# Moving the FFN's scaled float16 copy from ScalarE to GpSimd in a fused attention + FFN kernel

## The reference

```
xn = (x - mean) / sqrt(var + 1e-5)
attention: z = layernorm(xn)*g + b;  q = z Wq + bq, k = q, v = z Wv + bv
           16 heads of 16 channels; softmax(q k^T / 4) v;  times Wo, + bo
ffn:       h = gelu(xn ternary(W1) + b1)        256 -> 1024
           h ternary(W2) + b2                   1024 -> 256
```

## Time and profile before

| | us |
|---|---|
| median of 3 runs | 1436.96 (1436.22 to 1437.12) |
| profiled execution, device time | 1435.52 |
| its span, first to last instruction | 1433.7 |
| TensorE busy | 1384.6 (97%) |
| VectorE busy | 1339.1 (93%) |
| ScalarE busy | 1247.3 (87%) |
| GpSimd busy | 113.7 (8%) |

### The profile page before, as it was taken

The page is one execution under the profiler, slowest core; times in us unless marked ns, Lnnn a source line. Parts: engine busy times, 40 slices in busy tenths (PEclk is TensorE's granted clock), DMA queues, the critical chain, the costliest instruction groups (busy, mean ns, idle before and its releaser), DMA issues.

```text
span 1433.7 us, 32248 instructions
## 1 busy us (share of the span) xinstructions
PE 1384.6 (97%) x13414; PEld 447.5 (31%) x13414; DVE 1339.1 (93%) x1430; ACT 1247.3 (87%) x2284; POOL 113.7 (8%) x246
## 2 busy tenths in 40 slices
PE   7899987999999999999999999999999999999999
PEld 5666542222222222222222222222222222222244
DVE  7868779999999999999999999999999999999934
ACT  5554643999999999999999999899999999999975
POOL 2000005000000000000000000000222200002200
PEclk8999999999999999999999999999999999999999
DMA  6012000010000000100000001001212101001122
GB/s 232 16 36 76 30 16 1 28 31 30 31 31 31 30 31 30 31 30 26 29 30 29 32 29 33 28 32 35 60 61 61 61 31 33 32 33 60 39 100 81
DMA packets 28531, 60.69 MB, mean 42 GB/s; under 512 B 6200, under 2 KB 11736, under 8 KB 28130
## 3 DMA queue, kind: packets, MB, share of 16 engines
q1 hardware_dynamic: 27810, 56.99, 11.8%
q10 hardware_dynamic: 576, 1.65, 0.3%
HBM read 41.29 MB, written 16.77 MB: 40 GB/s over the span
## 4 chain that ended last, share of the span: by engine, by line
DVE 71%; PE 23%; ACT 2%; DMA 2%; issue 1%; POOL 0%; SPq 0%; ACTq 0%; DVEq 0%
DVE part_max L839 68%; PE ps L367 6%; PE ps L384 3%; PE ps L1070 3%; PE ps L1139 3%; PE ps L330 2%; PE ps L1085 2%; PE ps L458 1%; DVE w L831 1%; ACT w L1020 1%; DMA rows<-in_rows 1%; PE ps L439 1%; ACT hidden L1015 1%; PE ps L1111 1%; ACT w L1049 1%
## 5 line engine op out<-in xcount | busy, mean ns | idle before, releaser
L1049 ACT ACTIVATE w<-ps 128x512 f32<-128x512 f32 x2048 | 1111.4, 596 | 63.8 <-PE ps L384 21.6
L839 DVE TENSOR_REDUCE part_max<-ps 128x1 f32<-128x1024 f32 x1024 | 1164.8, 1211 | 1.9 <-PE ps L330 1.7
L367 PE MATMUL ps<-w,v_ones 128*32 128x256 f32 (+1 forms) x7688 | 628.6, 399 | 0.4
L384 PE MATMUL ps<-qry,key 50*128 50x512 f16 x1984 | 411.4, 388 | 7.2 <-ACT w L1049 7.0
L330 PE MATMUL ps<-qry,key 48*128 48x512 f16 x2048 | 404.2, 380 | 11.4 <-DVE part_max L839 11.3
L367 PEld LDWEIGHTS ps<-w,v_ones 128*32 128x32 f32 x7688 | 152.2, 108 | 384.7 <-issue 211.5
L384 PEld LDWEIGHTS ps<-qry,key 50*128 50x128 f16 x1984 | 101.1, 93 | 440.7 <-ACT w L1049 412.5
L330 PEld LDWEIGHTS ps<-qry,key 48*128 48x128 f16 x2048 | 101.5, 95 | 36.8 <-DVE part_max L839 26.4
L638 POOL COPY v_ones<-v_all 128x128 f32<-128x128 f32 x64 | 18.6, 291 | 743.9 <-PE ps L367 743.9
L1011 ACT ACTIVATE q_split<-ps,sigma_bq 128x512 f16<-128x512 f32 x16 | 11.0, 687 | 65.2 <-PE ps L1085 65.2
L1070 PE MATMUL ps<-w_ternary,w 128*128 128x256 f16 x512 | 61.7, 277 | 6.2 <-DVE w L831 6.2
(11 more groups left out here) (144 smaller groups left out, 466.2 us busy)
## 6 DMA issues: line engine op xcount, KB each, us to landing
key<-q_parts SPq DMA_DIRECT2D x64, 128.0 KB
qry<-q_parts SPq DMA_DIRECT2D x64, 128.0 KB
o_heads<-o_evacuated SPq DMA_DIRECT2D x31, 256.0 KB, 10.2
resid<-in_x SPq DMA_DIRECT2D x8, 512.0 KB, 13.8
q_parts<-q_split SPq DMA_DIRECT2D x16, 256.0 KB, 2.5
key<-q_parts SPq DMA_DIRECT2D x64, 64.0 KB
qry<-q_parts SPq DMA_DIRECT2D x64, 64.0 KB
out<-resid SPq DMA_DIRECT2D x7, 512.0 KB, 3.1
```

The costliest lines, as they stand in the source:

```text
L367: mm = eng.matmul(pv[32 * c:32 * c + 2 * D, c0:c1], vst[:, kb, :], prob[kb % 2][:, c * BANK + c0:c * BANK + c1], start=(kb == 0), stop=(kb ...
L384: eng.matmul(ring_bank(v, i, False), key[v][r:r + KROWS, kb * P:(kb + 1) * P], qry[v][r:r + KROWS, c * BANK:(c + 1) * BANK], start=True, s ...
L839: dve.tensor_reduce(part_max[h % 2][:, a // 2, a % 2:a % 2 + 1], pa[a % 2], AX.X, ALU.max).then_inc(s_r, 1)
L1049: act.activation(prob[kb % 2][:, c * BANK:(c + 1) * BANK], ring_bank(k, i, last), ACT.Exp, scale=exp_scale).then_inc(s_e, 1)
```

## The change

ScalarE's 32 copies at L1020, with their waits, are taken out. GpSimd writes the same float16 copy with a `tensor_scalar` multiplication by the column `hs`, one for each pair of blocks, and signals the same semaphore `s_h1`. Its stream is put in a new order: in the loop over the groups, `rsqrt(g + 1)` comes first, then the four copies of group g; the two `stage` copies of head 0 follow those of group 4. VectorE's, TensorE's and SyncE's streams stay as they are.

```
+            def hidden_part1(g):
+                for i in range(KF // 2):
+                    pool.wait_ge(s_g, KF * g + 2 * i + 2)
+                    if g == 0 and i == 0:
+                        pool.wait_ge(s_wd, 4)
+                    pool.tensor_scalar(hp[0][:, 2 * i:2 * i + 2, :], hid[:, 2 * i:2 * i + 2, :], hs[:, 0:1], None,
+                                       ALU.mult).then_inc(s_h1, 1)
...
-            for g in range(1, NG):
-                rsqrt(g)
...
-            pool.wait_ge(s_vd, 2 * NG // NB)
-            stage(0, 0)
-            stage(0, 1)
+            for g in range(NG):
+                if g + 1 < NG:
+                    rsqrt(g + 1)
+                hidden_part1(g)
+                if g == NG // NB:
+                    pool.wait_ge(s_vd, 2 * NG // NB)
+                    stage(0, 0)
+                    stage(0, 1)
             split_max(0)
...
                     act.activation(hid[:, f, :], pf[f % 2], ACT.Gelu, scale=1.0 / XS, bias=b1_col[:, f:f + 1]).then_inc(s_g, 1)
-                    if f % 2:
-                        if first and f == 1:
-                            act.wait_ge(s_wd, 4)
-                        act.wait_ge(s_g, KF * g + f + 1)
-                        act.activation(hp[0][:, f - 1:f + 1, :], hid[:, f - 1:f + 1, :], ACT.Identity,
-                                       scale=hs[:, 0:1]).then_inc(s_h1, 1)
```

## The result

The changed kernel takes **1464.35 us** (median of four runs, 1463.86 to 1466.55) against 1436.59 on the same chip: +27.8 us, a ratio of 1.0196 with a 95% interval from 1.0178 to 1.0214. The forecast was 1440.3, the range 1435 to 1462. The profiled execution of after took 1466.55 us; its span is 1464.6 against 1433.7.

The account below looks back on a forecast made before the run. The prediction took group 0 as bound by VectorE, groups 1 to 3 by the Gelu-and-copy chain, groups 4 to 6 by a chain leaving at Gelu 5. Terms 2.5 + 0.3 + 0.3 + 0.2 = +3.3 us gave 1440.3, range 1435 to 1462.

Parts of the forecast that it names:

- What bounds the kernel: First 240 us: TensorE sees 0.7 us of the copy tail in groups 1 to 3; VectorE is group 0's chain.
- The price of the added instruction: GpSimd's float32-to-float16 tensor_scalar of 128x1024: taken as 1.1 us, between bounds of 1.04 and 2.13 us.
- Who meets whom: GpSimd copies and VectorE's second parts, both using SBUF, would run in turn; each group 0 meeting costs VectorE up to 0.85 us.
- Groups 1 to 3: FFN down +0.1 us later each, +0.3 in all: 0.5 us won on ScalarE is lost in taking turns.
- Order and queues: GpSimd's new order costs nothing: 17.9 us idle before each pow on the mean, 9 left even at 2.13 a copy.
- Groups 4 to 7: Second part 2 +0.1 us later in each of groups 4 to 6, +0.3; two such links in group 7, +0.2.
- Group 0: Copies beside VectorE's norm, ternary weights and second parts: three meetings counted, +2.5 us; 0 at the lower end.
- the first: Rival for all eight groups: arithmetic rate, 2.13 us a copy in turn with second parts, +27 us, 1464; chance 0.13.
- a rival: Faster: second part reaches TensorE's limit, group 0's FFN down loses its 1.3 us low-clock stretch; -3.5 us, 1433.5; chance 0.05.

Follow-up runs that it names:

- e11: Kernel before, idle matmuls ahead of group 0's FFN down and transposes behind groups 4 to 6, third-pair copy of groups 1 to 3 as GpSimd tensor_copy, scale 1: 1429.75 us.
- e1: Kernel before, with one extra GpSimd instruction in each of seven heads where GpSimd is idle, results unread, to price each alone: 1433.35 us, run once.
- e2: Changed kernel with hidden scale set to 1 and a plain tensor_copy on GpSimd instead of the tensor_scalar: 1437.62 us against 1436.22 for the kernel before.
- e8: Changed kernel with scale 1 and tensor_copy on GpSimd, each pair copied twice, first to a scratch: 1465.69 us, ratio 1.0219.
- e12: Changed kernel with scale 1 and tensor_copy on GpSimd, two scratch fills that read nothing ahead of each copy: 1476.09 us, ratio 1.0285.
- e9: Changed kernel with 28 idle matmuls on TensorE ahead of FFN down of groups 1 to 3 only: 1461.01 us.
- e4: Kernel before, with only group 0's four float16 copies moved to GpSimd: 1438.58 us against 1436.22, ratio 1.0016.
- e3: Changed kernel, with group 0's four float16 copies back on ScalarE: 1460.39 us.
- e10: Kernel before, with 24 idle matmuls ahead of FFN down of group 0 and 12 ahead of the transposes behind groups 4 to 6: 1431.78 us against 1436.09.
- e5: Changed kernel with 28 idle matmuls on TensorE ahead of FFN down of groups 0 to 5: 1466.89 us.

## Why the prediction was wrong

- *What bounds the kernel*: right. The tail of 0.7 us in groups 1 to 3 was what could be had (e11 has 0.46 of it a group), and VectorE was the chain of group 0.
- *The price of the added instruction*: **the step that failed.** "I take 1.1, near the cast, because the new instruction too reads one tensor with those types" is wrong, and so is the upper bound of 2.13: I had taken two inputs as the costliest case. By itself the instruction takes 2852 ns (e1). With the price that I had assumed e2 is at +1.4 us (interval -0.9 to +3.2) where the sum said +3.3: within the forecast's own range, though not term by term, as group 0 lost 2.0 in place of 2.5 and got 1.3 back from the clock.
- *Who meets whom*: right in kind. In e8 second part and copy each wait for the other by 0.75 to 0.87 us, near the 0.85 of streaming time that I had priced. It was the wrong place to look: in groups 1 to 3 GpSimd's time for a pair and the slow start behind it give the whole loss (e12).
- *Groups 1 to 3*: said +0.1 each. With the cheap copy -0.2 (e2), with the real one +4.6 in groups 2 and 3: 3.0 of waiting for GpSimd, shown by e9 with the clock kept, and 1.6 for the clock. In group 1 it is +1.7, because FFN down of group 0 had been slow before and is not now.
- *Order and queues*: right that the new order costs nothing (e2). But the 9 us that even 2.13 us a copy would leave were counted over a whole group, and the copies only fit between Gelu 1 and FFN down.
- *Groups 4 to 7*: said +0.5, measured 16.5 in the profile, of which 5.1 are the clock (2.6, 1.4 and 1.2 above). That copies of 2.83 us put the chain on the first copy instead of Gelu 5 follows from the price. How much VectorE's stretched second parts (2.13 and 1.68 us in the chain of group 4) add was not tried apart. e12 without them, at 3.0 us a pair, took 11.7 us from Gelu 1 to the transposes, the changed kernel 11.5; an estimate from these two is 11.7 - 3 x 0.17 = 11.2 without the stretch, so 0.3 of the 2.1 us of a group.
- *Group 0*: said +2.5; FFN down came 3.4 late, and e4 gives +2.4 for it alone in the time of the kernel. Here the meetings are the cause: the four instructions for `xn`, 1.39 us in the earlier trace rows, took 2.88, and the four for `zn`, 1.29 before, took 2.85, together 3.0 of the 3.4.
- *Rivals*: the first gave 1464 and the time is 1464.35, by sums that agree partly by chance: it had a pair at 2.13 + 1.43 = 3.56 us in turns; measured were 2.83 without turns, group 0 at 3.4 in place of 6.5, the lower clock on top, and groups 4 to 7 dearer than it said. The estimate from the GPSIMD Engine Reference of the Trainium skill (Performance versus the Vector engine), 1.54 us by 1.8 cycles an element, was nearer than mine, but still about half of what e1 shows; its advice to keep elementwise arithmetic off this engine is borne out here (2852 ns against the 1148 of ScalarE).
- *TensorE's clock* stood only in a rival, as a gain that needed a shorter pause ahead of FFN down of group 0. That gain of 1.3 us came: the pause was 0.75 us, because VectorE's delay now fell ahead of the transposes, and these began slowly (8 of them in 1.94 us, 1.04 in the earlier trace rows):

```profile
40.94 1.94 PE L1116 MATMUL ps<-ident_f,xn 128*128 128x128 f32 x8 [5.30 <-DVE out_bound L821]
...
47.12 7.16 PE L1075 MATMUL ps<-w_ternary,w 128*128 128x256 f16 x64 [0.75 <-DVE w L842]
```

As a loss, some 8.5 us in groups 2 to 6 of the profiled execution, the clock had no term in the sum.

## What to carry to other kernels

Before work is moved to an idle engine, that engine's price for the very operation has to be known: a row of another operation with the same shapes and types can be off by 2.7 times, and one run with the instruction placed where the engine idles gives it. What counts then is the instruction's time against the time between two of them: with a copy of 1.04 us, less than the 2.4 us between pairs of Gelus, all the waiting on each other cost nothing that the time of the kernel shows (e2), while at 2.83 and 3.0 us each tenth counted four times a group. That the engine idles for half of the group does not help, when its work has to fit into one part of it. A pause ahead of a stage of matmuls can have a second price, a slow start behind it; it did not come each time (in e3 FFN down of group 3 took 7.16 us behind a pause of 3.7 us, those of groups 1 and 2 took 8.83 behind the same). Filling pauses with idle matmuls won 4 us in e10, and put 3 us into the chain where there was no pause (e5).

## What the runs showed of the hardware

The `tensor_scalar` on GpSimd takes 2852 - 1565 = 1287 ns for 512 more elements, 2.5 ns an element, three times the 0.83 of the copy. Why the multiplication is so slow no run shows. The timeline of group 0 in after shows when it keeps VectorE's norm waiting:

```profile
30.12 2.85 POOL L632 TENSOR_SCALAR w<-hidden,hidden_scale 128x1024 f16<-128x1024 f32 x1
...
30.24 1.14 DVE L734 TENSOR_SCALAR xn<-resid,mean_var,rstd 128x256 f32<-128x256 f32 x1 [0.30 <-POOL rstd L621]
31.30 0.72 DVE L734 TENSOR_SCALAR xn<-resid,mean_var,rstd 128x256 f32<-128x256 f32 x2
...
31.95 1.17 DVE L734 TENSOR_SCALAR xn<-resid,mean_var,rstd 128x256 f32<-128x256 f32 x1
```

Of the norm's instructions, 0.41 us each in the earlier trace rows, the one at the copy's start and the one towards its end take 0.7 to 0.8 us more; the two in between run undisturbed. The second part, which reads two tensors from SBUF, was held once beside such a copy, by 2.13 - 1.28 = 0.85 us. So an instruction of 2.85 us on GpSimd did not keep VectorE waiting for its whole length.

The Trainium skill (SBUF — State Buffer, Who interferes with whom) says that a VectorE instruction with two SBUF inputs contends with a GpSimd instruction that reads SBUF and not with one that only writes it, and that a VectorE instruction in a two-port mode contends with GpSimd. e12 agrees with the first: the second parts stayed at 1283 ns beside the fills. The norm's four instructions took 5.21 us instead of 1.39 beside four fills and one copy (2.00 beside a copy alone, in e2), so fills do delay these; that they run in a two-port mode no row shows.
